# Row maxima as sixteen columns, written into the query operand by DMA

## The reference

```
scores = einsum('bqhd,bkhd->bhqk', Q, K) / sqrt(8)
a = softmax(scores, axis=-1)          # exp(score - row maximum), divided by its sum
o = einsum('bhqk,bkhd->bqhd', a, V)
```

## Time and profile before

| quantity | value |
|---|---|
| time, median of 3 runs | 449.32 us |
| profiled execution, span from first to last instruction | 456.6 us |
| the profiled execution's own time | its span is the only time it left |
| PE busy | 372.2 us, 82% |
| DVE busy | 312.9 us, 69% |
| ACT busy | 291.9 us, 64% |
| POOL busy | 156.9 us, 34% |
| chain that ended last, by engine | PE 57%, DVE 16%, issue 10%, ACT 5%, POOL 5%, DMA 3% |
| mean granted TensorE clock | 0.923 |

### The profile page before, as it was taken

One profiled execution on the slowest core, in us unless ns is written; L12 is line 12 of the kernel. 1 busy time (PEld: TensorE's weight loads), 2 busy tenths in 40 slices (PEclk: granted clock), 3 DMA queues, 4 the chain that ended last, 5 costly groups with the idle time before them and its releaser, 6 DMA issues.

```text
span 456.6 us, 8815 instructions
## 1 busy us (share of the span) xinstructions
PE 372.2 (82%) x2122; PEld 249.3 (55%) x2122; DVE 312.9 (69%) x1071; ACT 291.9 (64%) x664; POOL 156.9 (34%) x196
## 2 busy tenths in 40 slices
PE   4587889999999899899999976888699567999700
PEld 2235546646546645556565553447547556999600
DVE  7325657788788688688788777656835675566446
ACT  3274597698698489569669665647865724555314
POOL 8333121232432342422532422322143164455522
PEclk9779899999999899899999998599959989999955
DMA  7613214313423432340450447611334013221053
GB/s 199 174 55 72 48 43 112 108 38 87 144 52 75 132 74 54 111 117 1 108 155 17 107 127 224 203 36 43 86 125 129 13 41 91 59 56 31 20 184 92
DMA packets 33001, 41.59 MB, mean 91 GB/s; under 512 B 4794, under 2 KB 24111, under 8 KB 32952
## 3 DMA queue, kind: packets, MB, share of 16 engines
q1 hardware_dynamic: 30680, 36.79, 30.3%
q0 software_dynamic: 2272, 4.24, 2.9%
HBM read 13.66 MB, written 14.79 MB: 62 GB/s over the span
## 4 chain that ended last, share of the span: by engine, by line
PE 57%; DVE 16%; issue 10%; ACT 5%; POOL 5%; DMA 3%; SPq 1%; DVEq 1%; POOLq 0%; ACTq 0%
PE bank L672 11%; PE bank L767 7%; PE bank L754 6%; PE bank L659 5%; PE bank L683 5%; PE bank L640 4%; PE bank L604 3%; POOL dispatched L1258 3%; PE bank L639 3%; PE bank L605 2%; PE bank L696 2%; DVE ca_nm L977 2%; ACT sa_qm L837 2%; PE bank L647 2%; DMA sa_pt<-results 1%
## 5 line engine op out<-in xcount | busy, mean ns | idle before, releaser
L896 ACT ACTIVATE sa_us<-bank,expert_b 128x128 f32<-128x128 f32 x156 | 44.3, 368 | 37.6 <-PE bank L754 22.2
L1238 POOL TENSOR_SCALAR_AFFINE_SELECT sa_pt<-sa_pt 128x512 f32<-128x512 f32 x64 | 39.4, 640 | 66.6 <-ACT sa_pt L845 66.3
L1263 POOL DMA_INDIRECT results<-sa_us,sa_pt x39 | 40.3, 1033 | 63.4 <-DVE sa_us L1173 53.5
L977 DVE TENSOR_REDUCE sa_nm<-bank 128x4 f32<-128x512 f32 x64 | 41.7, 683 | 13.6 <-PE bank L640 13.1
L754 PE MATMUL bank<-xsT,sa_pt 128*128 128x128 f32 x312 | 43.4, 284 | 5.2 <-DVE xsT L1160 3.4
L837 ACT CAST sa_qm<-bank 8x512 fp32r<-8x512 f32 x64 | 36.8, 576 | 16.4 <-PE bank L647 15.1
L767 PE MATMUL bank<-sa_over_qm,sa_us 128*128 x312 | 44.7, 288 | 2.9 <-ACT sa_us L896 1.7
L754 PEld LDWEIGHTS bank<-xsT,sa_pt 128*128 128x128 f32 x312 | 38.6, 195 | 8.6 <-DVE xsT L1160 5.4
L845 ACT ACTIVATE ca_pt<-bank 77x512 f32<-77x512 f32 x64 | 34.5, 595 | 12.1 <-PE bank L659 10.6
L767 PEld LDWEIGHTS bank<-sa_over_qm,sa_us 128*128 128x128 f32 x312 | 39.5, 198 | 4.8 <-issue 4.1
L845 ACT ACTIVATE sa_pt<-bank 128x512 f32<-128x512 f32 x64 | 34.8, 596 | 10.1 <-PE bank L659 10.0
(11 more groups left out here) (216 smaller groups left out, 846.6 us busy)
## 6 DMA issues: line engine op xcount, KB each, us to landing
dispatched<-filler SPq DMA_DIRECT2D x17, 520.0 KB, 4.5
sa_km<-sa_ku SPq DMA_DIRECT2D x32, 128.0 KB, 2.4
sa_qm<-sa_qu SPq DMA_DIRECT2D x32, 96.0 KB
ca_qm<-ca_qu SPq DMA_DIRECT2D x32, 96.0 KB
sa_pt<-dispatched SPq DMA_DIRECT2D x39, 65.0 KB
ca_km<-ca_ku SPq DMA_DIRECT2D x32, 77.0 KB, 2.1
sa_over_km<-in_e_w SPq DMA_DIRECT2D x1, 2048.0 KB, 8.6
sa_pt<-results SPq DMA_DIRECT2D x8, 256.0 KB, 5.2
```

Of the source, the lines that this page charges most:

```text
L896: act.activation(hid[n % 2][:, c, :], bank[b][:, P * (c if n < EARLY else c % 2):][:, 0:P], ACT.Gelu, bias=b1[:, bass.ds(expert * FC + c, ...
L977: dve.tensor_reduce(k.nm[:, u, g, :], bank[home_of(p)[k, "scores", u][g % 2]][:, :].rearrange("q (j n) -> q j n", j=J)[:, :, 0:k.keys], AX ...
L1263: pool.indirect_dma_start(out=results, out_offset=bass.IndirectOffsetOnAxis(ap=xs[n % RING][:, P:P + 1].bitcast(I32), axis=0), in_=ys[n % ...
```

## The change

The maxima go another way into `qm`. PE turns `nm` itself (128 queries by 16 heads, now laid out head block by group), so that 16 partitions hold one head each. ACT copies that into `mt` as the rounded part (one instruction), DVE subtracts it from the PSUM original and writes the rest into `mt`, and SP writes both by two DMAs a unit into row 0 and row 1 of `qm`, over all 16 heads (16 runs of 512 bytes each). The ones in `ku` move to rows 0 and 1 for every group. `weights` waits for the DMAs in place of ACT's copies.

```diff
-        c[:, 3 * P + g] = (row % 32 < 8) & (row % GROUPS == g)
+        c[:, 3 * P + g] = row < 2
...
-            k.nm = t("nm", [P, 2, GROUPS, J])
-            k.mm = t("mm", [P, 2, J, 32], F32R)
+            k.nm = t("nm", [P, 2, J, GROUPS])
+            k.mt = t("mt", [HEADS, 2, 2, P], F32R)
...
+            def shift(k, p, u):                                        # SP
+                if not after_pair(p) and u == 0:
+                    sp.wait_ge(k.s_zero, 2)
+                sp.wait_ge(k.s_mt_hi, p * 2 + u + 1)
+                sp.wait_ge(k.s_mt_lo, p * 2 + u + 1)
+                if after_pair(p):
+                    sp.wait_ge(k.s_s2_ps, (p - 1) * 8 + 4 * u + 4)
+                for h in range(2):
+                    dst = k.qm[h:h + 1].rearrange("r j g n -> r (j g) n")[:, :, P * u:P * u + P]
+                    sp.dma_start(dst.bitcast(F32), k.mt[:, u, h, :].bitcast(F32)).then_inc(k.s_shift[u], 16)
...
             def shift(k, p, u):                                        # PE
-                pe.wait_ge(k.s_mm, p * 2 + u + 1)
+                pe.wait_ge(k.s_nm, p * 8 + 4 * u + 4)
...
             def weights(k, p, part):                                   # PE
-                pe.wait_ge(k.s_sha, p * 8 + 4 * u + 4)
+                if half == 0:
+                    pe.wait_ge(k.s_shift[u], p * 32 + 32)
...
             def shift(k, p, u):                                        # ACT
-                for j in range(J):
-                    ...
-                    act.copy(k.qm[rows, j, :, P * u:P * u + P], src).then_inc(k.s_sha, 1)
+                act.copy(k.mt[:, u, 0, :], bank[home_of(p)[k, "shift", u][0]][0:HEADS, 0:P]).then_inc(k.s_mt_hi, 1)
...
             def shift(k, p, u):                                        # DVE
-                dve.tensor_copy(k.mm[:, u, :, 0:4], nm).then_inc(k.s_mmh, 1)
-                dve.wait_ge(k.s_mmh, p * 2 + u + 1)
-                dve.tensor_tensor(k.mm[:, u, :, 4:8], nm, k.mm[:, u, :, 0:4].bitcast(F32), ALU.subtract).then_inc(k.s_mm, 1)
+                dve.wait_ge(k.s_mt_hi, p * 2 + u + 1)
+                ...
+                dve.tensor_tensor(k.mt[:, u, 1, :], bank[home_of(p)[k, "shift", u][0]][0:HEADS, 0:P], k.mt[:, u, 0, :].bitcast(F32), ALU.subtract).then_inc(k.s_mt_lo, 1)
```

More of the change, by code:

```diff
@@ L207, in kind @@
             k.s_nm = sem(f"{name}_nm")
-            k.s_mmh = sem(f"{name}_mmh")
-            k.s_mm = sem(f"{name}_mm")
             k.s_mt_ps = sem(f"{name}_mt_ps")
-            k.s_sha = sem(f"{name}_sha")
+            k.s_mt_hi, k.s_mt_lo = sem(f"{name}_mt_hi"), sem(f"{name}_mt_lo")
+            k.s_shift = [sem(f"{name}_shift{u}") for u in range(2)]
             k.s_s2_ps = sem(f"{name}_s2_ps")
@@ L279, in build @@
         s_spread, s_cast = sem("spread_ready"), sem("constants_cast")
-        SETUP = 12
+        SETUP = 10
         block = stack.enter_context(nc.Block())
@@ L526, in rows @@
                 load(n)
-            iterations({"fill": fill, "turn": turn, "fetch": fetch, "spread_keys": spread_keys, "spread_terms": spread_terms, "first_layer": first_layer, "second_layer": second_layer, "rows": rows})
+            iterations({"fill": fill, "turn": turn, "fetch": fetch, "spread_keys": spread_keys, "spread_terms": spread_terms, "shift": shift, "first_layer": first_layer, "second_layer": second_layer, "rows": rows})
             sp.wait_ge(s_spare, 16)
@@ L644, in shift @@
             def shift(k, p, u):
-                pe.wait_ge(k.s_mm, p * 2 + u + 1)
+                pe.wait_ge(k.s_nm, p * 8 + 4 * u + 4)
                 take(home_of(p)[k, "shift", u][0])
-                pe.transpose(bank[home_of(p)[k, "shift", u][0]][:, 0:P], k.mm[:, u].rearrange("q j r -> q (j r)").bitcast(F32), ident).then_inc(k.s_mt_ps, 1)
-                give(home_of(p)[k, "shift", u][0], k.s_sha, p * 8 + 4 * u + 4)
+                pe.transpose(bank[home_of(p)[k, "shift", u][0]][0:HEADS, 0:P], k.nm[:, u].rearrange("q j g -> q (j g)"), ident).then_inc(k.s_mt_ps, 1)
+                give(home_of(p)[k, "shift", u][0], k.s_mt_lo, p * 2 + u + 1)
             def weights(k, p, part):
                 u, half = divmod(part, 2)
-                pe.wait_ge(k.s_sha, p * 8 + 4 * u + 4)
+                if half == 0:
+                    pe.wait_ge(k.s_shift[u], p * 32 + 32)
                 if part == 0:
@@ L828, in shift @@
             def shift(k, p, u):
-                if not after_pair(p):
-                    act.wait_ge(k.s_zero, 2)
                 act.wait_ge(k.s_mt_ps, p * 2 + u + 1)
                 if after_pair(p):
-                    act.wait_ge(k.s_s2_ps, (p - 1) * 8 + 4 * u + 4)
-                for j in range(J):
-                    rows = slice(32 * j, 32 * j + 8)
-                    src = bank[home_of(p)[k, "shift", u][0]][rows, 0:P].rearrange("r (o n) -> r o n", o=1).to_broadcast([8, GROUPS, P])
-                    act.copy(k.qm[rows, j, :, P * u:P * u + P], src).then_inc(k.s_sha, 1)
+                    act.wait_ge(k.s_shift[u], p * 32)
+                act.copy(k.mt[:, u, 0, :], bank[home_of(p)[k, "shift", u][0]][0:HEADS, 0:P]).then_inc(k.s_mt_hi, 1)
             def weights(k, p, part):
@@ L925, in _ @@
                 setup(dve.memset(k.vo[:, :, :, 32:64], 1.0))
-                setup(dve.memset(k.mm[:, :, :, :].bitcast(F32), 0.0))
             setup(dve.memset(CA.hk[:, 2 * SC:].bitcast(F32), 0.0))
@@ L973, in scores @@
                 if after_pair(p) and half == 0:
-                    dve.wait_ge(k.s_mm, (p - 1) * 2 + u + 1)
+                    dve.wait_ge(k.s_mt_ps, (p - 1) * 2 + u + 1)
                 for g in (2 * half, 2 * half + 1):
                     dve.wait_ge(k.s_s1_ps, p * 8 + 4 * u + g + 1)
-                    dve.tensor_reduce(k.nm[:, u, g, :], bank[home_of(p)[k, "scores", u][g % 2]][:, :].rearrange("q (j n) -> q j n", j=J)[:, :, 0:k.keys],
+                    dve.tensor_reduce(k.nm[:, u, :, g], bank[home_of(p)[k, "scores", u][g % 2]][:, :].rearrange("q (j n) -> q j n", j=J)[:, :, 0:k.keys],
                                       AX.X, ALU.max, negate=True).then_inc(k.s_nm, 1)
             def shift(k, p, u):
+                dve.wait_ge(k.s_mt_hi, p * 2 + u + 1)
                 if after_pair(p):
-                    dve.wait_ge(k.s_mt_ps, (p - 1) * 2 + u + 1)
-                dve.wait_ge(k.s_nm, p * 8 + 4 * u + 4)
-                nm = k.nm[:, u].rearrange("q g j -> q j g")
-                dve.tensor_copy(k.mm[:, u, :, 0:4], nm).then_inc(k.s_mmh, 1)
-                dve.wait_ge(k.s_mmh, p * 2 + u + 1)
-                dve.tensor_tensor(k.mm[:, u, :, 4:8], nm, k.mm[:, u, :, 0:4].bitcast(F32), ALU.subtract).then_inc(k.s_mm, 1)
+                    dve.wait_ge(k.s_shift[u], p * 32)
+                dve.tensor_tensor(k.mt[:, u, 1, :], bank[home_of(p)[k, "shift", u][0]][0:HEADS, 0:P], k.mt[:, u, 0, :].bitcast(F32), ALU.subtract).then_inc(k.s_mt_lo, 1)
             def restore(k, p, part):
```

## The result

The changed kernel took 491.8 us (median of 4 runs, 491.53 to 493.76) against 449.1 before: a ratio of 1.093 (95% interval 1.088 to 1.098), so 42.7 us slower where 25 were forecast. Run again beside the experiments, the pair gave 492.1 and 450.2. These and all later times are medians of a kernel's runs without those few in which the chip fell into a slower state, over 1.5% above the fastest.

What follows compares the result with a forecast made beforehand. PE's in-order list was taken to bound the kernel. Six passes at 3.0 us (18), the first pass 2 and the end 5 made 25 us, so 474 us from 449.3; 8-in-10 range 456 to 490.

Steps and rivals of the forecast that it cites:

- The end: Last part: SA shift behind first_layer's load 3.7 us late, 2 given back, slot table 2, last pair 1; 5 us slower.
- Net 3.0 us a pass: Passes with both attentions: holds cost 3.7 us, earlier turn and lighter DVE return 0.7; six passes give 18 us.
- The start: Stretch before the five middle passes: 2 us for the opening pass plus 3 for the first with both attentions.
- What goes: Work removed: ACT loses 2.0 us a unit, 65 over 32, buying little; DVE saves 0.2 a unit; turn starts earlier.
- The path: From maxima to landed transfers: 0.28 us ACT, 0.28 DVE, 0.6 SP issue, 2.0 landing; 3.2 us against 2.8.
- DVE is held: DVE's subtraction waits for PE's turn and ACT's copy, delaying steps behind; four units cost 3.7 us a pass.
- The first pass: Opening pass: longer path and loads ahead on SP show, some 1 us for each of two units; 2 us.
- Rival 1: DVE's holds are absorbed and only late DMAs count: 12 us slower, 461 us; chance 0.20.
- Rival 2: PE's clock also falls after idle stretches in each of six passes: 10 us more, 484 us; chance 0.20.
- Rival 3: Faster: holds meet idle time, DMAs land before weights, PE's waits before the turn shrink; at most -14, 440 us; chance 0.06.
- Rival 4: No change, because gains and holds cancel: 449 us; chance 0.04.
- What would show it: Profile signs: ACT 65 us less busy, DVE waiting about 1 us 32 times, PE's DMA waits before weights, 39 us passes.

Runs made afterwards that it cites:

- the control: The kernel before, unchanged, run again for a second profile: 450.2 us, profile span 448.4 us.
- both controls: The kernel before and the changed kernel, each unchanged, run again for a second profile: 450.2 and 492.1 us.

## Why the forecast was wrong

The direction, the mechanism and nearly all prices of instructions were right; the size was not. The step that failed is "The end. ... Together 5": it measured 17.0 us in two profiles at like pace, 12 of the 17.7 us that the forecast missed. The second is "Net 3.0 us a pass": the five passes cost 4.0 each, 5.1 us more than forecast. The start, forecast at 5, cost 2.1, which gives 2.9 back. The remaining 3.5 are the distance between the two profiles (39.2) and the timed runs (42.7).

- *What goes.* ACT lost 65.0 us as said. That it buys little is shown, not only argued: 0.4 us a pass, in two kernels.
- *The path.* 0.25, 0.28, 1.20 for two issues, 1.8 to 2.2 to land: as said, where no large transfer stands ahead.
- *DVE is held.* 1.2, 0.7, 0.9 and 0.9 us a pass were taken; PE's waits read 0.82, 0.95, 0.96 and 0.91 + 1.65. The four sum to 5.3 instead of 3.7, the late transfer behind `fill` being the term that was cut too short: I let it end at the fill's data and left out that SP issues late and slowly behind it (2.42 us for the two issues, 3.7 and 4.1 to land). Before's own waits here, 0.9 us a pass in the control (4.4 in five), come off: 4.4 by these rows, 4.0 by the length of the passes, where 3.0 were forecast. The holds alone are 3.6 of the 5.3, and they went with the subtraction (18.2 us in five passes fell to 1.9).
- *The first pass.* 2 forecast. The stretch up to the third pair, which also holds the first of the six passes (3 more), measured 2.1. Transfers cost PE 6.1 us there, but its 5.1 us of waits in front of the turn and for ACT's copies went, for which the forecast gave nothing back in the first pass.
- *The end.* The stall behind `first_layer` was foreseen at 3.7 and is 4.95. The same situation in the same queue recurs at `second_layer` (4.40), and I did not look for it; nor for the 1.91 us of the unit ahead of that load. With nothing awaited the end falls by 10.0 us; with DVE's hold gone as well by another 6.0, to before's level. I took 2 us for the hold of the slot table and 1 for the last pair, and 2 as given back in front of the turn (7.4 us there fell to 4.1).
- *Rival 1* (holds absorbed): refuted by 16.3 us of gain without them. *Rival 2* (the clock falls): not in the passes, where the granted clock is 1.00 in both controls; at the end it is, 0.85 for 0.88, and PE's busy time grew by 4.3 us (by 2.2 between the first two profiles). The place and the size were wrong, the mechanism was there: the clock of the end rose again to 0.90 in the run with neither hold nor landing, and it fell in the passes too (0.96, 6.8 us) once the transfers came later still. The stretch of the earlier trace rows itself was a wait for DVE's `ca_y`, not for a transfer.
- *Rival 3* (faster) needed a landing under 1 us; in the second profile of after the shortest took 1.7. With hold and landing both away the kernel is 7 us faster than before, but the kernel before with one rounding shows that a gain of this size needs no transfers at all.
- *Rival 4* (no change) falls with the times. *What would show it* came out in every point, passes of 39 us too, with longer waits than said: 1.6 us for about one in front of the subtraction, 4.95 for 3 to 4 in the last self-attention pair.

## What to carry to other kernels

Before you put a small transfer in a queue, walk that queue from start to end and list every large load ahead of it; each such pair can be a stall, and here the one that was found was not the only one. A step whose input comes from another engine holds all that its own engine has behind it, so a cheap instruction (0.28 us) cost 16 us over its 32 units here; and work taken off an engine that is idle a fifth of a pass (65 us of ACT) was worth almost nothing. Ask whether the value is needed: a softmax takes any shift, so the rounded maximum alone would do, and that cut was the one that paid (442.7 us).

## What the runs showed of the hardware

- A queue of its own does not shield a small transfer from a large load: 8 KB issued by ACT 0.6 us after 2048 KB of SP's landed after 6.1 us, against 1.8 at the median and 1.8 for the same transfer when the load was held back.
- SP's issuing itself was slower behind a large transfer: 2.42 us for two issues right behind the fill (two of 520 KB), 1.20 without.
- 8 KB from 16 partitions into a single partition landed in 1.8 us, hardly sooner than the 2.1 us of 77 KB.
